# Value products of an attention kernel from fp16 halves, on one core

## The reference

```
h = layernorm(x);  k = h @ Wk.T;  v = r = h @ Wr.T
y = wkv_scan(-exp(time_decay), time_first, k, v)     # recurrence along time
x = x + (sigmoid(r) * y) @ Wo.T

h = rmsnorm(layernorm(x), gamma1)
q = (h @ Wq + bq)                  -> b t H HD        # H = 16 heads of HD = 32
kv = ((h @ Wdown + bdown) @ Wup + bup) -> k, v        # latent of 64
att = softmax(einsum('bthd,btgd->bthg', q, k) / sqrt(HD))   # 16 x 16 for each token
out = einsum('bthg,btgd->bthd', att, v)
z = layernorm(x) + (out @ Wo + bo)
h2 = rmsnorm(z, gamma2);  gate = softmax(h2 @ Wg + bg)
x = x + z + sum_e gate_e * (h2 @ We_e)                # E = 8 experts of 512 x 512
```

## Time and profile before

| | |
|---|---|
| median of three runs | 2970.51 us |
| profiled execution | 2970.13 us, span 2968.3 us |
| granted PE clock, mean | 0.975 |
| PE busy | 2786.5 us, 94% |
| DVE busy | 2170.1 us, 73% |
| ACT busy | 1294.7 us, 44% |
| POOL busy | 610.0 us, 21% |
| value products (line 1231), PE | 267.9 us busy, 2048 records |

### The profile page before, as it was taken

The page is one execution under the profiler, slowest core; times in us unless marked ns, Lnnn a source line. Parts: engine busy times, 40 slices in busy tenths (PEclk is TensorE's granted clock), DMA queues, the critical chain, the costliest instruction groups (busy, mean ns, idle before and its releaser), DMA issues.

```text
span 2968.3 us, 47758 instructions
## 1 busy us (share of the span) xinstructions
PE 2786.5 (94%) x18896; PEld 1761.5 (59%) x18896; DVE 2170.1 (73%) x4100; ACT 1294.7 (44%) x2399; POOL 610.0 (21%) x681
## 2 busy tenths in 40 slices
PE   3269999999999999999999999999999999999989
PEld 2146566666666656666665566666556666656644
DVE  4887777877777777777777777777777777787753
ACT  1364454444444444444443444444344445344431
POOL 0122222122222212222221222122122122221210
PEclk9569999999999999999999999999999999999999
DMA  7012221112222112222211122221121221021110
GB/s 216 15 22 30 29 36 28 32 29 30 37 29 36 28 31 30 29 37 29 36 30 29 30 29 37 29 36 30 29 30 29 37 30 36 24 33 25 30 22 15
DMA packets 579074, 102.44 MB, mean 35 GB/s; under 512 B 547346, under 2 KB 547474, under 8 KB 578834
## 3 DMA queue, kind: packets, MB, share of 16 engines
q1 hardware_dynamic: 578852, 99.39, 19.4%
HBM read 48.49 MB, written 16.78 MB: 22 GB/s over the span
## 4 chain that ended last, share of the span: by engine, by line
PE 83%; DVE 6%; SPq 5%; DMA 2%; ACT 2%; issue 1%; POOL 0%; ACTq 0%; DVEq 0%
PE bank L1075 69%; PE bank L1231 8%; PE bank L1105 3%; SPq L439 3%; DVE mcol L987 3%; PE bank L1221 2%; DMA ks<-k 2%; SPq L435 2%; PE bank L1191 1%; ACT t L637 1%; PE bank L1208 1%; DVE mx L725 1%; DVE zz L915 0%; DVE w_e L823 0%; SPq L392 0%
## 5 line engine op out<-in xcount | busy, mean ns | idle before, releaser
L1075 PE MATMUL bank<-w_e,h2t 128*128 128x512 f16 x6144 | 1390.8, 382 | 5.3 <-DVE acc L1055 5.3
L1075 PEld LDWEIGHTS bank<-w_e,h2t 128*128 128x128 f16 x6144 | 598.8, 99 | 686.5 <-issue 17.5
L1055 DVE SCALAR_TENSOR_TENSOR acc<-bank,gates,acc 128x512 f32<-128x512 f32 x512 | 368.0, 729 | 246.3 <-PE bank L1075 245.7
L657 ACT ACTIVATE pr<-bank,col 128x512 f32<-128x512 f32 x256 | 171.6, 683 | 560.7 <-PE bank L1221 560.7
L1231 PE MATMUL bank<-vp,pr 128*128 128x33 f32 x2048 | 267.9, 276 | 5.1 <-ACT pr L657 5.0
L1231 PEld LDWEIGHTS bank<-vp,pr 128*128 128x128 f32 x2048 | 260.1, 196 | 17.3 <-DVE rden L1000 3.6
L476 POOL TENSOR_TENSOR zz<-wkv,zz 128x512 f32<-128x512 f32 x64 | 105.2, 1644 | 772.0 <-DVE ev L902 772.0
L1075 PE MATMUL bank<-w_o,xo 128*128 128x512 f16 x768 | 174.7, 385 | 55.6 <-DVE xo L853 55.6
L915 DVE RECIPROCAL zz<-zz 128x256 f32<-128x256 f32 x128 | 223.1, 1743 | 0.0
L987 DVE TENSOR_REDUCE mcol<-bank 128x4 f32<-128x512 f32 x256 | 155.9, 680 | 39.0 <-PE bank L1208 39.0
L1075 PE MATMUL bank<-w_o,qo 128*128 128x512 f16 x768 | 173.9, 384 | 6.4 <-DVE qo L853 6.4
(11 more groups left out here) (178 smaller groups left out, 3713.3 us busy)
## 6 DMA issues: line engine op xcount, KB each, us to landing
qs<-qo SPq DMA_DIRECT2D x384, 64.0 KB, 3.4
xk<-in_attn_x SPq DMA_DIRECT2D x32, 512.0 KB, 3.7
x<-in_attn_x SPq DMA_DIRECT2D x32, 512.0 KB, 3.7
result<-acc SPq DMA_DIRECT2D x32, 512.0 KB, 2.8
ks<-k SPq DMA_DIRECT2D x128, 64.0 KB, 3.3
w_e<-in_ffn_We SPq DMA_DIRECT2D x7, 1024.0 KB, 14.1
qs<-in_attn_Wk SPq DMA_DIRECT2D x1, 1024.0 KB, 5.8
ks<-in_attn_Wr SPq DMA_DIRECT2D x1, 1024.0 KB, 7.9
```

The lines of the kernel that those rows point to most:

```text
L657: nc.scalar.activation(pr[:, k % 2, :], att_bank[ATT_BANK["S", k]][:, :], ACT.Exp, scale=colof["soft"])\
L1055: V.scalar_tensor_tensor(out=acc[:, s, :], in0=moe_bank[u % 2][:, :], scalar=gates[:, s, e:e + 1], in1=acc[:, s, :], op0=ALU.mult, op1=ALU ...
L1075: ins = nc.tensor.matmul(dst, left(a), right(b), start=(n == 0), stop=(n == last))
```

## The change

The probabilities and the values are split into f16 halves too, and the value products of a group become two f16 products instead of one f32 product: the high half of the probabilities times [values high, ones, values low, zeros] (66 columns), and the low half of the probabilities times [values high, ones] (33 columns), added in PSUM to the first.

- ACT evaluates the exponential twice, into pr (f32) and into the high half pr16 (f16), scaled by 4096 through a bias.
- POOL gets a new piece att_scores: it subtracts the high half from pr and writes the low half of pr16. PE's att_probs waits for it.
- DVE transposes v into hrow (f32) instead of vp; ACT copies that as f16 into vp (new piece att_vt on ACT); DVE writes the low half (new piece att_vlo).
- In att_probs DVE first adds the two blocks of 32 columns with a reduction, then multiplies by the reciprocal in place, from hrow.
- The scale of the values moves into bvs, and constants replace two scale columns. The scratch for dynamic transfers is set to 2048.
- The lists of PE, DVE, ACT and POOL are new; SP's is the same.

```diff
@@ orders (two of the new rows; the lists are otherwise permuted)
+    ("att_max", 2), ("att_max", 3), ("moe", 6), ("att_m", 0), ("moe", 7), ("att_scores", 0), ("att_scores", 1),
+    ("att_m", 0), ("mix_value", 0), ("mix_scan", 0), ("moe", 6), ("moe", 7), ("mix_rec", 0), ("mix_rec", 1),
...
@@ tiles
-        vp = sb("vp", [P, G, HD + 1])
+        vt32 = on
+        vp = sb("vp", [P, G, VW], F16)
+        pr16 = sb("pr16", [P, 2, 2, 4 * P], F16)
+        plog = sb("plog", [P, 1])
...
@@ POOL
+            def att_scores(t, k):
+                pool.wait_ge(*att_act.done(t, "ex", 2 * k + 1))
+                if k >= 2:
+                    pool.wait_ge(*att_pe.done(t, f"PV{k - 2}"))
+                nc.gpsimd.tensor_tensor(pr16[:, 1, k % 2, :], pr[:, k % 2, :], pr16[:, 0, k % 2, :], ALU.subtract).then_inc(att_pool.sem, 1)
...
@@ ACT
-                nc.scalar.activation(pr[:, k % 2, :], att_bank[ATT_BANK["S", k]][:, :], ACT.Exp, scale=colof["soft"])\
+                nc.scalar.activation(pr[:, k % 2, :], att_bank[ATT_BANK["S", k]][:, :], ACT.Exp, bias=plog[:, 0:1], scale=colof["soft"])\
+                    .then_inc(att_act.sem, 1)
+                nc.scalar.activation(pr16[:, 0, k % 2, :], att_bank[ATT_BANK["S", k]][:, :], ACT.Exp, bias=plog[:, 0:1], scale=colof["soft"])\
                     .then_inc(att_act.sem, 1)
+
+            def att_vt(t, _):
+                act.wait_ge(*att_dve.done(t, "vt"))
+                nc.scalar.activation(vp[:, :, 0:HD], vt32, ACT.Copy).then_inc(att_act.sem, 1)
...
@@ DVE
-                V.transpose(vp[:, :, 0:HD], va32[:, :, :, :].rearrange("p g b j -> p g (b j)")).then_inc(att_dve.sem, 1)
+                V.transpose(vt32, va32[:, :, :, :].rearrange("p g b j -> p g (b j)")).then_inc(att_dve.sem, 1)
+
+            def att_vlo(t, _):
+                dve.wait_ge(*att_act.done(t, "v_hi"))
+                V.tensor_tensor(vp[:, :, HD + 1:2 * HD + 1], vt32, vp[:, :, 0:HD], ALU.subtract).then_inc(att_dve.sem, 1)
...
                 V.reciprocal(rden[:, 4 * k:4 * k + 4], pv[:, :, HD]).then_inc(att_dve.sem, 1)
-                dve.wait_ge(*att_dve.done(t, "norm", 2 * k))
-                V.tensor_tensor(on[:, 4 * k:4 * k + 4, :], pv[:, :, 0:HD],
-                                rden[:, 4 * k:4 * k + 4].unsqueeze(2).to_broadcast([P, 4, HD]), ALU.mult).then_inc(att_dve.sem, 1)
+                V.tensor_reduce(og, pv.rearrange("p g (l d) -> p g d l", l=2)[:, :, 0:HD, :], AX, ALU.add).then_inc(att_dve.sem, 1)
+                dve.wait_ge(*att_dve.done(t, "norm", 3 * k + 1))
+                V.tensor_tensor(og, og, rden[:, 4 * k:4 * k + 4].unsqueeze(2).to_broadcast([P, 4, HD]), ALU.mult).then_inc(att_dve.sem, 1)
...
@@ PE
-                pe.wait_ge(*att_act.done(t, "ex", k))
+                pe.wait_ge(*att_pool.done(t, "p_lo", k))
                 for n in range(4):
-                    ins = nc.tensor.matmul(att_bank[ATT_BANK["PV", k]][:, n * (HD + 1):(n + 1) * (HD + 1)],
-                                           pr[:, k % 2, n * P:(n + 1) * P], vp[:, 4 * k + n, :], start=True, stop=True)
+                    pv = att_bank[ATT_BANK["PV", k]][:, n * VW:(n + 1) * VW]
+                    nc.tensor.matmul(pv, pr16[:, 0, k % 2, n * P:(n + 1) * P], vp[:, 4 * k + n, 0:VW], start=True, stop=False)
+                    ins = nc.tensor.matmul(pv[:, 0:HD + 1], pr16[:, 1, k % 2, n * P:(n + 1) * P], vp[:, 4 * k + n, 0:HD + 1],
+                                           start=False, stop=True)
...
@@ kernel
-    nc = bacc.Bacc("TRN2", target_bir_lowering=False, num_devices=1)
+    nc = bacc.Bacc("TRN2", target_bir_lowering=False, num_devices=1, dynamic_dma_scratch_size=2048)
```

More of the change, by code:

```diff
@@ L36 @@
 XS = 2048.0
+PS = 4096.0
+OT = 8.0
 NEG_INF = -1e38
@@ L133 @@
 PE_ORDER = [
[L134 to L139, removed]
+    ("mix_turn", 0), ("moe", 0), ("mix_k", 0), ("att_turn", 0), ("moe", 1), ("att_latent", 0), ("att_q", 0),
+    ("att_up", 0), ("mix_v", 0), ("moe", 2), ("moe", 3), ("moe", 4), ("att_max", 0), ("att_max", 1), ("moe", 5),
+    ("att_max", 2), ("att_max", 3), ("moe", 6), ("att_m", 0), ("moe", 7), ("att_scores", 0), ("att_scores", 1),
+    ("moe", 8), ("att_probs", 0), ("att_scores", 2), ("att_probs", 1), ("att_scores", 3), ("moe", 9),
+    ("att_probs", 2), ("att_scores", 4), ("att_probs", 3), ("att_scores", 5), ("moe", 10), ("att_probs", 4),
+    ("att_scores", 6), ("att_probs", 5), ("att_scores", 7), ("moe", 11), ("att_probs", 6), ("att_probs", 7),
     ("moe", 12), ("moe", 13), ("att_project", 0), ("moe", 14), ("moe", 15), ("att_turn2", 0), ("mix_project", 0),
@@ L144 @@
 DVE_ORDER = [
[L145 to L153, removed]
+    ("mix_turn", 0), ("att_stats", 0), ("att_norm", 0), ("moe_gate", 0), ("att_turn", 0), ("moe", 0), ("moe", 1),
@@ new lines @@
+    ("att_latent", 0), ("mix_decay", 0), ("att_stack", 0), ("att_vt", 0), ("moe", 2), ("moe", 3), ("mix_sum", 0),
+    ("att_vlo", 0), ("moe", 4), ("att_max", 0), ("att_max", 1), ("att_max", 2), ("att_max", 3), ("moe", 5),
+    ("att_m", 0), ("mix_value", 0), ("mix_scan", 0), ("moe", 6), ("moe", 7), ("mix_rec", 0), ("mix_rec", 1),
+    ("mix_gate", 0), ("moe", 8), ("att_probs", 0), ("att_probs", 1), ("mix_split", 0), ("mix_decay", 1),
+    ("att_probs", 2), ("att_probs", 3), ("att_probs", 4), ("moe", 9), ("att_probs", 5), ("moe", 10), ("mix_sum", 1),
@@ L154 @@
+    ("mix_value", 1), ("moe", 11), ("att_probs", 6), ("att_probs", 7), ("att_back", 0), ("mix_scan", 1), ("moe", 12),
+    ("moe", 13), ("mix_rec", 2), ("att_project", 0), ("mix_rec", 3), ("mix_gate", 1), ("moe", 14), ("mix_split", 1),
+    ("pre_stats", 0), ("moe", 15), ("pre_norm", 0), ("att_turn2", 0), ("mix_project", 0),
 ]
 ACT_ORDER = [
-    ("mix_turn", 0), ("att_norm", 0), ("moe_gate", 0), ("moe", 0), ("att_turn", 0), ("moe", 1), ("mix_k", 0),
-    ("moe", 2), ("moe", 3), ("att_latent", 0), ("att_q", 0), ("att_up", 0), ("mix_v", 0), ("mix_exp", 0), ("moe", 4),
@@ L159 @@
[L159 to L163, removed]
+    ("mix_turn", 0), ("att_norm", 0), ("moe_gate", 0), ("att_turn", 0), ("mix_k", 0), ("moe", 0), ("moe", 1),
@@ L169 @@
+    ("att_scores", 6), ("att_scores", 7), ("mix_sum", 1), ("mix_num", 1), ("att_square", 0), ("moe", 15),
+    ("pre_stats", 0),
 ]
@@ L662, in att_back @@
                 for h in range(2):
-                    nc.scalar.activation(qo16[:, 0, HF * h:HF * h + HF, :], ot32[:, HF * h:HF * h + HF, :], ACT.Copy, scale=colof["ot_hi"])\
+                    nc.scalar.activation(qo16[:, 0, HF * h:HF * h + HF, :], ot32[:, HF * h:HF * h + HF, :], ACT.Copy, scale=OT)\
                         .then_inc(att_act.sem, 1)
@@ L802, in _ @@
             product(colof["t0"], p(C_), p("u"), 2.0 ** -17)
-            product(colof["vv"], p(C_), p("u"), 2.0 ** -28)
             product(colof["soft"], p(Q_), p(K_), 2.0 ** -22 * float(HD) ** -0.5)
-            times(colof["ot_hi"], i_(K_), 2.0 ** 14)
             product(colof["x2"], p(K_), p("o2"), 2.0 ** -28)
@@ L1059, in _ @@
                            "mix_project": mix_project, "att_stats": att_stats, "att_norm": att_norm,
-                           "att_turn": att_turn, "att_latent": att_latent, "att_stack": att_stack, "att_vt": att_vt, "att_max": att_max,
+                           "att_turn": att_turn, "att_latent": att_latent, "att_stack": att_stack, "att_vt": att_vt, "att_vlo": att_vlo, "att_max": att_max,
                            "att_m": att_m, "att_probs": att_probs, "att_back": att_back,
```

43 lines of the change are left out of this document (27 added, 16 removed).

## The result

The changed kernel takes 3135.15 us (median of 4 runs, 3130.89 to 3136.61), the kernel before 2969.08 (4 runs): a ratio of 1.055, 95% interval 1.052 to 1.058. It is slower by 166 us; the forecast was 135. The profiled execution took 3135.53 us, with a span of 3133.7.

The account below looks back on a forecast made before the run. The prediction took PE, busy 94%, to bound the kernel. Tile stages of 36.0 + 38.0 + 17.0 = 91.0 us against 86.5, +4.5 times 30 tiles, gave +135 us: 3105 us, range 2975 to 3205.

Parts of the forecast that it names:

- stage A: PE's span from a tile's first transposes to its maximum products: 36.0 us forecast (35.6 to 36.7), 36.8 in the profile.
- stage B: PE's span from the maximum products to the projection of the attention: 38.0 us forecast, where it was 33.1 to 33.2.
- Value products: On PE, a group of four heads falls from 0.81 to 0.24 us, a gain of 4.6 us a tile.
- The group on DVE: DVE's reduction and multiply for each group of value products: from about 0.42 to 0.76 us, the reduction being 0.41.
- The sign of a wait of 2 us in nearly every tile: Sign of being right: PE waits about 2 us for the copies of k in nearly every tile.
- POOL's price on DVE: POOL's subtractions and denominator sum slow DVE between the maxima and the attention output's transpose: 3.2 us a tile, 0 to 6.6.
- The reduction term: Eight added DVE reductions out of PSUM, one a group: 2.7 us a tile, from below 1.6, from above 5.4.
- POOL's latency: Low halves of the probabilities, ready about 2.5 us after their scores, make PE wait beside DVE's waits: nothing added.
- DVE blocked throughout: Rival: DVE is blocked for the whole of each POOL subtraction, +7.9 us a tile, 3207 us; chance 0.22.
- POOL free: Rival: POOL's subtractions cost DVE nothing, +1.3 us a tile, 3010 us; chance 0.18.
- The faster case: Rival: DVE's work slips into PE's waits after the maxima, -2.2 us a tile, 2904 us; chance 0.09.
- the upper end of 6.6 us: Most that POOL's work could cost DVE a tile, if each subtraction blocks DVE for nearly its whole length.

Follow-up runs that it names:

- high halves: Only the high f16 halves in the value products, low halves left out: 2864.97 us in the lists of the kernel before, 2917.41 in the changed kernel's lists.

## Why the prediction was right

The sign, the stage and the mechanism held; the sizes were 4.5 us a tile forecast and 5.7 measured in the tile shown. The total owes something to luck: stage A came out 0.9 us shorter than forecast and stage B 2.1 longer, and the two errors partly cancel.

- *Value products*: 0.24 us a group, measured 0.23. *The group on DVE*: reduction 0.41, measured 0.39.
- *Stage A*: 36.0, measured 35.1. The wait for the copies is 0.97, not 2.3, mostly since they land in 2.4 us, not 3.3. I had put the set-up at nothing for the transfers, and that was wrong. So was, for this kernel, that taking the unit out of A gains next to nothing: with the same products and the same landing A is 36.2 in the old lists and 34.7 in the new ones. It holds only where the copies land in 3.3, in the run with the lists alone (36.3). The sign of a wait of 2 us in nearly every tile came weaker: 0.8 us, in 23 of 29 tiles.
- *Stage B*: 38.0, measured 40.1. m is written 8.55 us into it, not 7.9: POOL's att_rest, moved ahead of mix_sum 0, falls on DVE's scans and low half of the values, and the reductions begin at 1570.73 though PE began the maxima at 1568.43. With att_rest late m comes at 7.9, as forecast. I had costed the low half at nothing, with DVE's spare time in A as cover, and att_rest's new place not at all; the account of the change has the lists move work in two places, and this is a third. From m to the transpose it is 28.3 us, forecast 26.6.
- *POOL's price on DVE* is the term that was mis-sized: "7 x 1.1 = 7.7 us, at 41% 3.2 us". Measured, 4.7. Of it 3.8 lie beside the subtractions. With an eighth of them DVE's scans and mix_decay's third step take 110 us less over the span, and 110 of the 166 us come back.
- *The reduction term* was 2.7 us a tile, 80 us. A group takes DVE 0.73 us where it took 0.43, so 2.4; but taken out alone the reductions are worth 22 us, and 41 with an eighth of the subtractions. The costs overlap, so single terms don't sum to the whole.
- *POOL's latency*: "I add nothing for them" was right; the run in which PE does not wait for POOL took as long.
- *The rivals*: DVE blocked throughout, 3207, was too high, POOL free, 3010, too low. The faster case asked for DVE under some 20 us between m and the transpose, and DVE had 28.
- *Not in the prediction*: the clock that falls behind PE's waits, and the lists' price. The lists cost 136 us with f32 products and 52 with high halves, and save 50 with both halves. Two of these are differences to a list that was never fitted to those products, the f32 number has the longer landing in it, and the old lists with both halves have att_rest late; how far a third list would bring both halves down stays open.

## What to carry to other kernels

Before work is moved to an idle engine, look at what its neighbour runs at those moments: the subtractions on a POOL that was 21% busy cost 110 us, about as much as the 104 us of work that PE saved, by shutting out DVE. A saving on the bounding engine counts only up to the next engine's sum in that stage; here that was 29.3 of 33.0 us. Judge an order list only with the products and the set-up it is to carry.

## What the hardware showed beyond expectation

Where DVE's scans or two-input operations and POOL's subtractions overlapped, most of the overlap was lost to one or the other. In the rows shown, from 1589.77 to 1592.10 (2.33 us), DVE lost 1.48 and POOL up to 3.12 - 2 x 1.16 = 0.80 (1.16 is its shortest). That agrees with the rule of the Trainium skill, page "SBUF — State Buffer", section "Who interferes with whom", that the later of two such operations waits for the whole of the earlier. Summed over the stage the price stayed under the upper end of 6.6 us. Two of the subtractions cost nothing: they lay beside DVE's pair of reciprocals (3.35 us at 1581.94, against 1.74 for one alone) and took 1.16 us each.

PE's granted clock fell to the lower level after some of its waits of 1.1 to 1.9 us between small products, and a unit of 2.75 us then took 4.37 to 4.45: such a wait costs twice. Not every one does it: after 1.60 us at 1581.42 and after 1.10 at 1597.70 the unit took 2.76. What decides, these runs do not show.
